# A batched conditional MLP with layer norm: residual and centring moved into the PSUM bank, the finish given to GpSimd and ScalarE, and the order of the first batches and of the end rewritten

## The reference

```python
out_nr  = gelu(x @ w1_nr + b1_nr) @ w2_nr + b2_nr                  # condition 0, NR
out_tsr = gelu(x @ w1_tsr + b1_tsr) @ w2_tsr + b2_tsr              # condition 1, TSR
h = gelu(x @ w1_sr + b1_sr)                                        # condition 2, SR: 1024 wide
out_sr  = gelu(h @ w2_sr + b2_sr) @ w3_sr + b3_sr
y = x + (out_nr, out_tsr or out_sr, by condition)
mu, var = mean(y), mean((y - mu) ** 2)                             # over the last axis
result = (y - mu) * rsqrt(var + 1e-5) * gamma + beta
```

## Time and profile before

| | before |
|---|---|
| three runs shown | 568.27, 566.2, 568.05 us; median 568.05 |
| profiled execution | 566.76 us, of which the span of its instructions is 564.9 |
| TensorE | 2409 matmuls, first of a batch at 5.43 us, last at 554.41 |
| busy | TensorE 97%, VectorE 54%, GpSimd 40%, ScalarE 35% |

### The profile page before, as it was taken

The page is one execution under the profiler, slowest core; times in us unless marked ns, Lnnn a source line. Parts: engine busy times, 40 slices in busy tenths (PEclk is TensorE's granted clock), DMA queues, the critical chain, the costliest instruction groups (busy, mean ns, idle before and its releaser), DMA issues. The chain is left out here.

```text
span 564.9 us, 8095 instructions
## 1 busy us (share of the span) xinstructions
PE 550.5 (97%) x2409; PEld 452.7 (80%) x2410; DVE 304.7 (54%) x476; ACT 195.3 (35%) x299; POOL 227.2 (40%) x165
## 2 busy tenths in 40 slices
PE   8989999999999999999999999999999999999992
PEld 5867888888888888888888888888888888888882
DVE  5792158967867878113810479312876016501765
ACT  5442143242342442324321442224144133413421
POOL 0979995753654554300330047300355100500155
PEclk9999999999999999999999999999999999999997
DMA  8844714354254444200410053300345002400042
GB/s 305 309 146 155 228 70 152 113 181 153 107 186 138 159 149 148 75 0 0 157 66 0 0 200 116 129 0 0 105 142 198 1 0 74 149 0 0 1 150 75
DMA packets 26223, 61.23 MB, mean 108 GB/s; under 512 B 3042, under 2 KB 3042, under 8 KB 26082
## 3 DMA queue, kind: packets, MB, share of 16 engines
q1 hardware_dynamic: 26208, 61.10, 31.2%
q10 hardware_dynamic: 2, 0.00, 0.0%
HBM read 44.31 MB, written 16.78 MB: 108 GB/s over the span
## 5 line engine op out<-in xcount | busy, mean ns | idle before, releaser
L433 DVE TENSOR_TENSOR g_lo<-bank,g_hi 128x512 fp32r<-128x512 f32 x112 | 76.5, 691 | 223.2 <-DVEq L123 222.8
L384 ACT ACTIVATE g_hi<-bank,bcol 128x512 fp32r<-128x512 f32 x112 | 77.7, 694 | 226.2 <-ACTq L123 225.3
L556 POOL TENSOR_TENSOR y<-y,row 128x512 f32<-128x512 f32 x64 | 101.1, 1598 | 84.7 <-POOLq L123 84.5
L560 POOL TENSOR_TENSOR rstd<-var_eps,power 128x2 f32<-128x2 f32 (+1 forms) x34 | 34.0, 1001 | 217.3 <-POOLq L123 217.3
L243 PE MATMUL bank<-w_hi,g_hi 128*128 128x512 f32 x256 | 99.6, 389 | 0.0
L244 PE MATMUL bank<-w_lo,g_hi 128*128 128x512 f32 x256 | 99.6, 389 | 0.0
L245 PE MATMUL bank<-w_hi,g_lo 128*128 128x512 f32 x256 | 99.6, 389 | 0.0
L243 PE MATMUL bank<-x_hi,w_hi 128*128 128x512 f32 x240 | 93.4, 389 | 1.1 <-PEq L123 1.1
L245 PE MATMUL bank<-x_hi,w_lo 128*128 128x512 f32 x240 | 93.4, 389 | 0.0
L244 PE MATMUL bank<-x_lo,w_hi 128*128 128x512 f32 x240 | 93.4, 389 | 0.0
L243 PE MATMUL bank<-g_hi,w_hi 128*128 128x512 f32 x192 | 74.8, 390 | 1.8 <-issue 1.8
(11 more groups left out here) (38 smaller groups left out, 605.6 us busy)
## 6 DMA issues: line engine op xcount, KB each, us to landing
y<-x SPq DMA_DIRECT2D x64, 256.0 KB, 3.5
out<-y SPq DMA_DIRECT2D x64, 256.0 KB, 2.8
stage<-x_t SPq DMA_DIRECT2D x31, 512.0 KB, 3.8
w_raw<-weights SPq DMA_DIRECT2D x17, 512.0 KB, 3.4
row<-rows SPq DMA_DIRECT2D x1, 1280.0 KB, 11.4
stage<-x_t SPq DMA_DIRECT2D x2, 256.0 KB, 3.9
w_raw<-weights SPq DMA_DIRECT2D x2, 256.0 KB, 4.5
cond_sb<-cond ACTq DMA_DIRECT2D x1, 0.1 KB
```

The source lines that it names most:

```text
L384: eng.activation(g_hi[:, slot, :], psum, ACT.Gelu, bias=b)
L433: eng.tensor_tensor(g_lo[:, slot, :], psum, g_hi32[:, slot, :], ALU.subtract).then_inc(s_gs, 1)
L556: eng.tensor_tensor(y[:, t, :], y[:, t, :], row[:, kind, :], ALU.add).then_inc(s_xb, 1)
L560: eng.tensor_tensor(rstd[:, t:t + n], var_eps[:, t:t + n], power[:, t:t + n], ALU.pow).then_inc(done, n)
```

## The change

- **In the bank.** `residual` writes into the bank, `stats` and `centre` read it there; only `centre` writes `y`. ScalarE raises `s_acc` once `centre` of a tile is done, and TensorE takes it bank by bank in SR.
- **Finish.** Outside the end, all four tiles are finished by ScalarE's copy and GpSimd's shift; VectorE's `finish` is gone there. GpSimd adds EPS itself, from a semaphore (`s_moments`) that VectorE raises behind a pair of moments.
- **GpSimd's order.** In batch 0 of kind NR, the second deviations stand between the halves of the first split; the two SR1 splits come right behind, then three of SR2, then all shifts. The four TSR splits stand behind the bias of batch 1 (they stood ahead of it), and ahead of the deviations of batch 1.
- **Hints.** TensorE's branches are written out, and the jump at the end of each kind carries a branch hint, marked at the kind's start.
- **Start.** 14 matmuls of 128x128 follow the nine warm-up matmuls; of the first chunks VectorE casts the weights and ScalarE x (it was mostly the other way). SyncE keeps two weight loads under way, where it had one.
- **End.** VectorE runs `centre` of tile 2 ahead of the residual of tile 3, GpSimd runs shift 2 ahead of the last `rstd`.

```diff
+N_WARM, N_WARM_SHORT = 9, 14
...
             for item in POOL_ALL:
-                eng.wait_ge(s_loaded[before], 16)
+                eng.wait_ge(s_loaded[landed[landed.index(item) - 2]], 16)
                 load_pair(item)
...
                 for j in range(4):
-                    if j == 2:
-                        take(eng, s_acc, 4)
+                    if j >= 2:
+                        take(eng, s_acc)
                     layer1(kind, j)
...
+            for _ in range(N_WARM_SHORT):
+                eng.matmul(bank[7][:, 0:P], ones[:, 0:P], ones[:, 0:P], start=True, stop=True)
...
+                def body(kind):
+                    with nc.body(f"tensor_kind_{kind}", valid_engines=[eng.engine]):
+                        ahead = eng.mark_branch_hint_location()
+                        step(kind, read_next)
+                        eng.br("tensor_kinds_end").branch_hint(ahead)
...
-                for t in range(FINISHED_BY_OTHERS_END if last else FINISHED_BY_OTHERS):
+                for t in range(FINISHED_BY_OTHERS_END if last else TT):
                     take(eng, s_v)
+                    if kind != NONE:
+                        eng.sem_inc(s_acc, 1)
                     take(eng, s_rstd)
                     eng.activation(y[:, t, :], y[:, t, :], ACT.Copy, scale=rstd[:, t:t + 1]).then_inc(s_n, 1)
...
-                    eng.tensor_tensor(y[:, t, :], bank[4 + t][:, :], y[:, t, :], ALU.add).then_inc(s_ev, 1)
+                    eng.tensor_tensor(bank[4 + t][:, :], bank[4 + t][:, :], y[:, t, :], ALU.add).then_inc(s_ev, 1)
...
-                eng.bn_stats(bn[:, t, :], y[:, t, :]).then_inc(s_bn, 1)
+                eng.bn_stats(bn[:, t, :], made_in(kind, t)).then_inc(s_bn, 1)
...
+            def centre(kind, t, done=s_v):
+                eng.scalar_tensor_tensor(out=y[:, t, :], in0=made_in(kind, t), scalar=mv[:, t, 0:1], in1=row[:, R_GAMMA, :],
                                          op0=ALU.subtract, op1=ALU.mult).then_inc(done, 1)
...
                     moments(kind, t + 1)
-                    variances(t, 2)
-                    centre(kind, t, s_v if t < FINISHED_BY_OTHERS else s_v_end)
-                    centre(kind, t + 1, s_v if t < FINISHED_BY_OTHERS else s_v_end)
-                for t in range(FINISHED_BY_OTHERS, TT):
-                    finish(kind, t)
+                    take(eng, s_mv, 2)
+                    eng.sem_inc(s_moments, 2)
+                    centre(kind, t)
+                    centre(kind, t + 1)
...
+            def deviations(t, n):
+                take(eng, s_moments, n)
+                eng.tensor_scalar(var_eps[:, t:t + n], mv[:, t:t + n, 1], EPS, None, ALU.add).then_inc(s_var, n)
                 take(eng, s_var, n)
+                eng.tensor_tensor(rstd[:, t:t + n], var_eps[:, t:t + n], power[:, t:t + n], ALU.pow).then_inc(s_rstd, n)
...
+                if kind == NR:
+                    deviations(0, 2)
+                    split_hi(POOL_SR[0])
+                    deviations(2, 2)
+                    split_lo(POOL_SR[0])
+                    for item in POOL_SR[1:6]:
+                        split(item)
+                    shift_all()
+                    for item in POOL_SR[6:]:
+                        split(item)
...
+            batch(eng, cond_of, 0, first)
+
+            batch(eng, cond_of, 1, bias)
+            with eng.If_cmp(cond_of_0, TSR, "IS_NE"):
+                for item in POOL_TSR:
                     split(item)
+            with eng.Fori(2, NBATCH - 1) as b:
+                deviations_of_all()
+                shift_all()
                 batch(eng, cond_of, b, bias)
```

More of the change, by code:

```diff
@@ L37 @@
 ORDER_SR = [(j, t) for j in range(2) for t in range(TT)] + [(j, t) for t in range(TT) for j in (2, 3)]
[L40 to L48, removed]
+FINISHED_BY_OTHERS_END = 3
+N_WARM, N_WARM_SHORT = 9, 14
 def conditional_mlp(nc, x, x_t, cond, weights, bias_cols, rows, out):
@@ L356, in step @@
                     if first < 4:
-                        eng.wait_ge(s_split["sr1"], 4)
-                        layer1(kind, first + 4)
-                        layer1(kind, first + 5)
+                        for j in (first + 4, first + 5):
+                            if j < 6:
+                                take(eng, s_acc)
+                            eng.wait_ge(s_split["sr1"], 4)
+                            layer1(kind, j)
                 eng.wait_ge(s_split["sr2"], 4)
@@ L411, in hi @@
                 eng.copy(dst, src).then_inc(s_first, 1)
[L413 to L415 removed]
+            for c in range(2):
+                hi(x_hi[:, c, :], stage[:, 0, c, :], s_x_piece[c])
             for c in (2, 3):
@@ L454, in moments, with variance @@
                 eng.bn_aggr(mv[:, t, :], bn[:, t, :]).then_inc(s_mv, 1)
[L456 to L461 removed]
+            def centre(kind, t, done=s_v):
+                eng.scalar_tensor_tensor(out=y[:, t, :], in0=made_in(kind, t), scalar=mv[:, t, 0:1], in1=row[:, R_GAMMA, :],
                                          op0=ALU.subtract, op1=ALU.mult).then_inc(done, 1)
+            def variance(t):
+                take(eng, s_mv)
+                eng.tensor_scalar(var_eps[:, t:t + 1], mv[:, t:t + 1, 1], EPS, None, ALU.add).then_inc(s_var, 1)
             def finish(kind, t):
@@ L542, in _, with split_hi @@
         def _(eng):
-            def split(item):
+            def split_hi(item):
                 c = pair(item)
@@ L564, in shift, with deviations_of_all, shift_all @@
                 eng.tensor_tensor(y[:, t, :], y[:, t, :], row[:, R_BETA, :], ALU.add).then_inc(s_fin, 1)
-            def finish():
-                deviations(0, 2, s_rstd)
-                shift(0)
-                shift(1)
-                deviations(2, 2, s_rstd_end)
+            def deviations_of_all():
+                for t in (0, 2):
+                    deviations(t, 2)
+            def shift_all():
+                for t in range(TT):
+                    shift(t)
             def bias(kind, read_next):
@@ L601, in _ @@
-            batch(eng, cond_of, 0, bias_first)
-            with eng.Fori(1, NBATCH - 1) as b:
+                if kind == NR:
[8 more added lines that the diff above has]
+                        split(item)
+                elif kind == SR:
+                    for item in POOL_SR:
+                        split(item)
+                    deviations_of_all()
+                    shift_all()
+                elif kind == TSR:
+                    for item in POOL_TSR:
+                        split(item)
+                    deviations_of_all()
+                    shift_all()
+                    for item in POOL_SR:
+                        split(item)
+                else:
+                    deviations_of_all()
+                    shift_all()
+                    for item in POOL_SR:
+                        split(item)
```

174 lines of the change are left out of this document (98 added, 76 removed).

## The result

| | before | after |
|---|---|---|
| runs shown | 567.27 us, median of 4 (566.2 to 568.27) | 562.11 us, median of 4 (561.57 to 562.6) |
| ratio | | 0.9909 (95%: 0.9884 to 0.9934) |
| profiled execution | 566.76, span 564.9 | 561.57, span 559.8 |
| TensorE, last matmul starts | 554.41 | 551.93 |
| span behind that start | 10.5 | 7.9 |

The change wins 5.2 us (567.27 - 562.11), 0.9%. The forecast was 3.3 us. Half of the gain is ahead of the last matmul (554.41 - 551.93 = 2.5 us), half behind it (2.6).

A forecast was written before the change was run, and what follows sets the result against it. The prediction took GpSimd's queue, delaying batch 1's second layer, to bound the kernel's end. Gains of 1.4 at the start and 1.9 at the end made 3.3 us: 564.7 against the 568.05 median, range 562.2 to 567.0.

The forecast's parts named there:

- 1.4 at the start: Batches 0 to 2: 3.7 us won by an earlier layer 2, less 2.3 us idle before batch 2's last layer.
- 1.9 at the end: Behind the last matmul: the last store's issue is over at 560.2 instead of 562.12, 1.9 us won.
- What bounds the kernel, and where the stall goes: GpSimd's queue delays batch 1's layer 2 (43.16 to 39.3), then batch 2's last layer (96.1, 2.3 us idle).
- two times add, wait and `pow`, 2 x 1.35: GpSimd behind batch 1's biases: from 89.4 to `rstd` 2 and 3 at 92.1.
- The 7.04 for the biases of batch 1: GpSimd's queue: four biases, with two `x_lo` of VectorE cutting into them, take 7.04 us as before.
- Hidden by GpSimd's chain: Hints, short warm-ups and swapped first casts move batch 1's start, but waits at 39.3 and 96.1 cover them: 0.
- 1.05 and 1.2: Worth in us of an earlier batch 1 start, without idle time and from the head, if the cover were gone.
- The bank is handed back ... 0: Steady batches: handing the bank back behind `centre` costs 0; SR first claims it at block 2, 5.4 us in.
- A: GpSimd's chain at least 2.3 us shorter than thought, TensorE alone counts: 5.6 us won, 562.4; chance 0.12.
- B: GpSimd's small add costs 1.03 like a `pow`, three in the chain: only 0.5 us stays, 567.5; chance 0.10.
- C: TensorE's clock falls in batch 2's 2.3 us of idle time, costing 1.6 us: 566.3; chance 0.07.
- D: Slower: the `y` loop makes `rstd` 3 late in seven short batches, 6.2 us lost, over 570.9; chance 0.04.

The follow-up runs named there:

- a3: Changed kernel with three unused GpSimd adds of 128x256 behind the TSR splits, ahead of the deviations of batch 1: 565.4 us, ratio to before 0.998.
- a5: Changed kernel with two TSR splits ahead of deviations 0 and 1, one ahead of 2 and 3, the last behind the shifts: 560.17 us, ratio to before 0.9886.
- after_again: The changed kernel once more, unedited, in the second session as yardstick: 561.97 us, ratio to before 0.992.
- b1: Kernel before with only residual, statistics and `centre` in the bank: 566.66 us, ratio to before 1.0003.
- a2: Changed kernel with the order of the end as before: 564.36 us, ratio to before 0.9956.
- b4: b3 with TensorE taking the banks one by one in SR: 563.98 us, ratio to before 0.9938.
- b5: b4 with TensorE's branches written out, the hints and the 14 short warm-ups: 561.94 us, ratio to before 0.9913.
- b3: Kernel before with the bank part and the new order of the end: 565.04 us, ratio to before 0.9977.
- a1: Changed kernel without the branch hints and the 14 short warm-ups: 562.1 us, ratio to before 0.9916.
- a6: a5 without the branch hints: 562.38 us, ratio to before 0.9928.
- a7: a5 without the 14 short warm-ups: 561.0 us, ratio to before 0.9896.

## Why the prediction was right in its mechanism and wrong in its sizes

The step that failed is the sum: its two terms, 1.4 at the start and 1.9 at the end, were both too small, and the 568.05 it was taken from was too high. The chain of waits was the one foretold.

**What bounds the kernel, and where the stall goes: right.** Nothing moved between 97 and the last matmul. The wait for VectorE's `finish` at 43.16 became a shorter wait at 39.05 (39.3 given), and a new one appeared in the middle of batch 2 behind GpSimd's TSR splits. a3 delays that queue, a5 shortens it, and the time follows in both. Batch 2 started at 82.76 (83.0 foretold) and hidden block 4 of batch 1 at 44.91 (44.9).

**The term of 1.4 at the start was mis-sized: 2.5 us.** The last layer of batch 2 starts at 95.05, not 96.1. Of the 1.1, 0.4 were there in batch 0 already (second `pow` over at 34.85, not 35.25), mostly because the biases of batch 0 ended at 29.02, where the sum held 29.32 fixed. GpSimd's first split had started at 13.90 where it was 14.38 in the profile of before, and that start moved between 13.77 and 14.89 from kernel to kernel. That part is luck of the one profile: after_again, with 14.32, starts layer 2 at the 39.3 foretold. Then the step "two times add, wait and `pow`, 2 x 1.35" is wrong: it is 2.19 (89.05 to 91.24). The add was too cheap (0.22, not 0.10), the `pow` too dear (0.71, not 1.03), since the price of before held a wait that the change removes. b1 shows that alone: with nothing but the bank changed the mean falls from 1.04 to 0.70. The other 0.2 are the way from `pow` to TensorE. The 7.04 for the biases of batch 1 came out right by another way: they took 5.03, and VectorE's `x_lo` cut into a TSR split instead (2.03 and 3.14 for 1.05 and 2.40).

**The term of 1.9 at the end was mis-sized: 2.6 us.** `finish` starts 4.30 behind the last matmul's start, where the sum had 4.6. And the last store lands sooner: in the profile of before it was issued at 561.75 and landed at 564.64, 2.9 us later, with store 2 just ahead of it; after it is 557.08 to 559.53, 2.45. The sum had moved the issue and kept the landing. a2, with store 2 just ahead, shows 2.9 again, but so do b4 and b5 (3.0 and 2.9) with store 2 issued 1.4 us earlier, so what makes a landing long stays open. The order of the end is worth 2.25 in the changed kernel (a2), and 1.6 beside b1 (b3).

**"Hidden by GpSimd's chain": right for this kernel, wrong as a price.** a1 shows that hints and warm-ups change nothing there. The text gave 1.05 and 1.2 if the cover were gone. b5 against b4 gives 2.0 for both, with overlapping intervals. a6 gives 2.2 for the hints alone by the medians, of which its profile accounts for 1 (its head was late for another reason). The unhinted turn left TensorE idle for 1.6 to 2.45 us in five later profiles, not the 1.05 of the profile of before. For the warm-ups the 1.2 were too low at batch 1's start (1.8 in a7 against a5) and too high at the end (0.8, not clear of noise). "The bank is handed back ... 0" holds only with the take bank by bank: with the old take of four, b1 shows two waits of 0.60.

**The rivals.** A names the side on which the miss lies (GpSimd's chain shorter) but not its mechanism: the `x_lo` did cut in. B is out (0.22). C's event was seen only in a3, behind 3.31 us of idle time. D is out: no gap in the batches 3 to 7 (its price counts seven short batches, where 3 to 7 are five and eight follow batch 2; nothing rests on it). The bound low enough for A was set against 568.05, the median of three runs; before's four medians are 566.29 to 567.27, so the whole range stood about 1 us too high: of the 2.6 between forecast and result, 0.8 are this (568.05 - 567.27) and 1.8 the two terms.

**Where the gain comes from.** By steps from before, each beside its own session: bank 0, the end 1.6, the take bank by bank 1.1 by the medians (2.2 by the ratios), hints and warm-ups 2.0 by the medians (1.4 by the ratios), and then the finish by others with GpSimd's new order about 0, where a5's order makes it 1.5 by the ratios (0.9913 to 0.9886). The intervals of b4 and b5 overlap, so how these 3 us divide between the take bank by bank and the hints and warm-ups is loose. The parts do not add up one by one, since each removes a wait that the next one shows. What remains open: how much the hints and the warm-ups win over many executions, and what the two-deep loads and the swapped casts do, which were not tried alone.

## What to carry to other kernels

An edit that is priced at nothing because something covers it should be written down with its cover: here the hints were worth 0 in the changed kernel and 1 to 2 us one reordering later, and the bank was worth 0 alone. Look for the instruction that is late next and move work behind it: moving the weight splits around the deviations and shifts won 1.8 us, beside 5.2 of the whole change. A first matmul that starts 1 us late in one profile can pass for an effect of the edit, so the head of each profile has to be read before two are compared. A duration read while a neighbour engine runs something that excludes it holds some of that neighbour's time, so a change that removes the neighbour makes it cheaper too.

## What the runs showed of the hardware

- **GpSimd and VectorE take turns.** GpSimd's `pow` of 128x2 took 1.04 us on average while VectorE's `centre` beside it read two SBUF tensors (all 30 of them 1.03 to 1.17), and 0.70 with one of them in the bank (b1, only the bank part changed); for 128x1 it is 0.89 and 0.90 beside such a `centre`, and 0.55 otherwise. VectorE's pair of `finish` takes 4.0 to 4.2 beside the splits, and 1.4 in the later batches (94.62 to 96.03 in the kernel before). The GPSIMD Engine Reference of the Trainium skill (section 1, Specifications) speaks of contention with VectorE instructions that have two SBUF inputs; the traces agree, and show that the loss falls on small GpSimd instructions as well.
- **The unhinted branch.** Without hints TensorE stood idle for 1.05, 1.63, 1.75, 2.19, 2.31 and 2.45 us at the turn from batch 0 to 1 in six kernels, and at none of the later turns; with hints there was no gap there. Runtime: NRT & Kernel Launch of the Trainium skill (section Instruction fetch mechanics) has a taken branch out of the loaded pages stall for a fetch. The first turn agrees with it; whether the targets of the 14 later turns, which show no gap, lay in the loaded pages no run here shows.
- **The clock at the start.** With the 14 short warm-ups TensorE reached 2.4 GHz between 3.4 and 6.4 us in all eight profiles, at the latest during the first real matmul. Without them it stood idle for 0.6 to 0.8 us behind the nine long ones and reached it at 9.0 to 9.9 in five profiles, behind eight to ten real matmuls 0.43 us apart, but in a1 ahead of the first real matmul. It varies by execution, so one profile cannot price the warm-ups.
- **The clock behind idle time.** It stayed at 2.4 GHz behind gaps of 1.2 to 2.45 us. Behind the 3.31 us in a3 it fell to 1.2 GHz from 99.0 to 102.4, which is one execution.
